# The experts' second layer with the hidden rows as the stationary operand

## The reference, cut to what matters

```python
a, g = jnp.split(xf @ We1[e] + be1[e], 2, axis=-1)
act = a * gelu(g)
yE  = act @ We2[e] + be2[e]          # the second layer, the place of the change
yr  = jnp.einsum('end,ne->nd', yE, w) # w: two weights of a row, the rest zero
x   = x + layernorm(ys + yr)
```

## Time and profile before

| what | us |
|---|---|
| three executions | 1189.19 median, 1187.93 to 1189.62 |
| the profiled execution, span | 1189.8 |
| PE busy | 1035.2 (87%) |
| DVE busy | 833.9 (70%) |
| ACT busy | 746.2 (63%) |
| POOL busy | 631.6 (53%) |
| 822 to 1091 us (pairs): PE, DVE, ACT busy | 268.29, 170.21, 173.46 of 269.00 |
| 1104 to 1130 us (singles): PE, DVE, ACT busy | 21.41, 18.47, 18.37 of 26.00 |

### The profile page before, as it was taken

The page is one execution under the profiler, slowest core; times in us unless marked ns, Lnnn a source line. Parts: engine busy times, 40 slices in busy tenths (PEclk is TensorE's granted clock), DMA queues, the critical chain, the costliest instruction groups (busy, mean ns, idle before and its releaser), DMA issues. The chain is left out here.

```text
span 1189.8 us, 31490 instructions
## 1 busy us (share of the span) xinstructions
PE 1035.2 (87%) x8446; PEld 597.5 (50%) x8446; DVE 833.9 (70%) x2411; ACT 746.2 (63%) x1311; POOL 631.6 (53%) x1184
## 2 busy tenths in 40 slices
PE   4689998898899898998777999866999999999875
PEld 3543333333333333332245665535888888888732
DVE  7587777777777777776768898532666666666737
ACT  4677767777767767775655566413666666666716
POOL 3246666666666666664422777771444444444344
PEclk9799999999999999998996899878999999999988
DMA  8313333333332333333243111112222222221166
GB/s 222 86 56 97 94 94 94 105 92 90 90 107 86 97 93 100 94 98 104 81 127 130 54 55 55 55 55 71 65 60 62 64 61 64 64 65 51 46 220 211
DMA packets 135606, 107.47 MB, mean 90 GB/s; under 512 B 32203, under 2 KB 127874, under 8 KB 135538
## 3 DMA queue, kind: packets, MB, share of 16 engines
q1 hardware_dynamic: 124722, 87.45, 26.1%
q0 software_dynamic: 8544, 17.78, 4.2%
q10 hardware_dynamic: 2272, 1.45, 0.4%
HBM read 55.96 MB, written 50.69 MB: 90 GB/s over the span
## 5 line engine op out<-in xcount | busy, mean ns | idle before, releaser
L1536 DVE TENSOR_REDUCE maxima<-ps 128x8 f32<-128x1024 f32 x320 | 384.3, 1222 | 125.4 <-PE ps L1159 111.1
L911 ACT ACTIVATE pT_area<-ps 128x1024 f32<-128x1024 f32 x320 | 327.7, 1026 | 143.6 <-PE ps L1190 143.0
L699 POOL TENSOR_SCALAR_AFFINE_SELECT pT_area<-pT_area 128x256 f32<-128x256 f32 (+1 forms) x448 | 190.8, 440 | 109.3 <-ACT pT_area L911 107.4
L801 POOL DMA_INDIRECT ys_dram<-quad_area,place_cur x139 | 133.1, 957 | 192.5 <-issue 136.6
L1231 PE MATMUL ps<-pT_area,quad_area 128*32 128x512 f32 (+3 forms) x2048 | 190.6, 446 | 0.0
L791 POOL DMA_INDIRECT xs_dram<-quad_area,idx_cur x128 | 123.0, 961 | 77.6 <-issue 75.2
L1190 PE MATMUL ps<-quad_area 64*128 64x512 bf16 (+3 forms) x1024 | 124.9, 301 | 37.3 <-DVE maxima L1536 34.7
L1398 PE MATMUL ps<-quad_area 128*128 128x256 f32 (+1 forms) x456 | 129.8, 367 | 6.3 <-issue 4.5
L1399 PE MATMUL ps<-quad_area 128*128 128x256 f32 (+1 forms) x456 | 128.3, 363 | 0.0
L1159 PE MATMUL ps<-quad_area 61*128 61x128 bf16 (+2 forms) x1792 | 126.4, 243 | 0.0
L1019 ACT ACTIVATE xnT<-ps,be_cur 128x256 f32<-128x256 f32 (+1 forms) x228 | 94.6, 448 | 47.6 <-PE ps L1399 47.3
(11 more groups left out here) (237 smaller groups left out, 1593.0 us busy)
## 6 DMA issues: line engine op xcount, KB each, us to landing
qk_dram<-split_area SPq DMA_DIRECT2D x192, 128.0 KB, 2.3
quad_area<-qk_dram SPq DMA_DIRECT2D x256, 96.0 KB, 2.3
row_area<-xs_dram SPq DMA_DIRECT2D x63, 132.0 KB, 2.1
pT_area<-ys_dram SPq DMA_DIRECT2D x16, 512.0 KB, 5.3
pT_area<-in_L_ffn_We SPq DMA_DIRECT2D x12, 384.0 KB, 6.1
out_dram<-pT_area SPq DMA_DIRECT2D x7, 512.0 KB, 2.9
xs_dram<-row_area SPq DMA_DIRECT2D x5, 528.0 KB, 4.2
split_area<-in_L_ffn_We SPq DMA_DIRECT2D x12, 192.0 KB, 3.6
```

What stands on the lines that cost most here:

```text
L699: return pool.affine_select(out=blocks, in_=blocks, compare_op=ALU.is_ge, fill=0.0, base=0, pattern=[[0, count], [1, P]], channel_multipli ...
L801: pool.indirect_dma_start(ys_dram, at, ys[:, ns % 2, h, :], None).then_inc(s_yst[ns % 2], 16)
L911: act.activation(pT[:, gs % 2, n, :], ps[:, bank:bank + 2, :].rearrange("p a b -> p (a b)"), ACT.Exp).then_inc(s_exp, 1)
L1536: dve.tensor_reduce(to, ps[:, bank:bank + 2, :].rearrange("p a (j k) -> p a j k", k=P), AX, ALU.max).then_inc(s_mxf, 1)
```

## The change

The operands of the second layer are exchanged. `hidT` (128 columns of it, one half of the tile) is now stationary and a 128 x 128 piece of `w2_cur` moves, so the result has rows on partitions at once. A pair takes six products of 128 columns instead of three of 256, a single three of 128. The two transposes of a pair, ACT's copy to `ysT` and `ysT` itself are gone; banks 6 and 7 (`Y_BANKS`) hold the results of alternate tiles.

With rows on partitions the bias is a row that is the same on all of them. `be2_all` holds the twelve rows on all 128 partitions, loaded by one broadcast DMA of 6 KB for each partition behind the expert weights; a new DVE copy brings the tile's row to `be2_cur`. `weigh` is DVE's new last step on a result: an addition of the bias (PSUM to SBUF, L1842 of the changed kernel), a wait until that is finished, and a product with the weights (SBUF to SBUF, L1844). `weigh(n-2)` stands ahead of the register load and of both copies, where before the product stood behind them. `beT` and `be_cur` lose a column, and `yT` moves to make room.

```diff
+            sp.dma_start(be2_all, a["L0_ffn_be2"].rearrange("(o e) c -> o (e c)", o=1).broadcast_to([P, E * C])).then_inc(s_we, 16)
...
-                if 0 <= ns - 1 < ROUTED:
-
-                    act.wait_ge(s_yeT, n)
-                    w = width(ns - 1)
-                    act.activation(ysT[:, (ns - 1) % 2, 0:w], ps[:, YT_BANK, 0:w], ACT.Identity,
-                                   bias=be_cur[:, (ns - 1) % 8, 6:7]).then_inc(s_yeTsb, 1)
...
                     pe.wait_ge(s_w2c, n)
-                    ge(pe, s_yeTsb, n - 1)
+                    ge(pe, s_yeb, n - 2)
                     for k in range(CHUNKS):
                         pe.wait_ge(s_hide, CHUNKS * (n - 1) + k + 1)
-                        last = pe.matmul(ps[:, YT_BANK, 0:w], w2_cur[:, par, k * P:(k + 1) * P], hidT[:, par, k, 0:w],
-                                         start=(k == 0), stop=(k == CHUNKS - 1))
-                    last.then_inc(s_yeT, 1)
-                if 0 <= ns - 2 < ROUTED:
-
-                    pe.wait_ge(s_yeTsb, n - 1)
-                    ge(pe, s_yesb, n - 2)
-                    for h in range(halves(ns - 2)):
-                        last = pe.transpose(ps[:, Y_BANK, h * P:(h + 1) * P], ysT[:, ns % 2, h * P:(h + 1) * P], ident[:])
+                        for h in range(halves(ns - 1)):
+                            last = pe.matmul(ps[:, Y_BANKS[par], h * C:(h + 1) * C], hidT[:, par, k, h * P:(h + 1) * P],
+                                             w2_cur[:, par, k * C:(k + 1) * C], start=(k == 0 and h == 0),
+                                             stop=(k == CHUNKS - 1 and h == halves(ns - 1) - 1))
                     last.then_inc(s_ye, 1)
...
-                    ge(dve, s_yeT, n - 1)
+                if 0 <= ns - 2:
+                    weigh(ns - 2, n - 2)
+                if ns < ROUTED:
+                    ge(dve, s_ye, n - 1)
                     e = dve.value_load(etile[0:1, bass.ds(n, 1)], min_val=0, max_val=E - 1)
                     dve.tensor_copy(w2_cur[:, par, :], we2[:, bass.ds(e * HR, HR)]).then_inc(s_w2c, 1)
-                if 0 <= ns - 2:
-
-                    par, h = ns % 2, halves(ns - 2)
-                    dve.wait_ge(s_ye, n - 1)
-                    wait_apart(dve, s_wt, 5 * n - 5, s_passed)
-                    if ns >= 4:
-                        dve.wait_ge(s_yst[par], stored(ns - 4, n - 4))
-                    dve.tensor_tensor(ys[:, par, 0:h], ps[:, Y_BANK, 0:P * h].rearrange("p (h c) -> p h c", h=h),
-                                      weight_cur[:, (ns - 2) % 4, 0:h].rearrange("p (h o) -> p h o", o=1).broadcast_to([P, h, C]),
-                                      ALU.mult).then_inc(s_yesb, 1)
+                    dve.tensor_copy(be2_cur[:, par, :], be2_all[:, bass.ds(e * C, C)]).then_inc(s_b2c, 1)
+
+            def weigh(ns, n):
+
+                par, h = ns % 2, halves(ns)
+                to, w = ys[:, par, 0:h], weight_cur[:, ns % 4, 0:h]
+                bias = be2_cur[:, par].rearrange("p (o c) -> p o c", o=1).broadcast_to([P, h, C])
+                dve.wait_ge(s_ye, n + 1)
+                wait_apart(dve, s_b2c, n + 1, s_passed)
+                wait_apart(dve, s_wt, 5 * n + 5, s_passed)
+                if ns >= 2:
+                    dve.wait_ge(s_yst[par], stored(ns - 2, n - 2))
+                dve.tensor_tensor(to, ps[:, Y_BANKS[par], 0:C * h].rearrange("p (h c) -> p h c", h=h), bias, ALU.add).then_inc(s_yeb, 1)
+                wait_apart(dve, s_yeb, n + 1, s_passed)
+                dve.tensor_tensor(to, to, w.rearrange("p (h o) -> p h o", o=1).broadcast_to([P, h, C]), ALU.mult).then_inc(s_yesb, 1)
```

More of the change, by code:

```diff
@@ L59 @@
 XS_BANKS = (4, 5)
-YT_BANK, Y_BANK = 6, 7
+Y_BANKS = (6, 7)
 PICK_STEPS, BOTH_STEP, PLACE_STEPS = 13, 12, 10
@@ L219, in build @@
         v_flat = v_all[:].rearrange("p t c -> p (t c)")
-        yT = v_flat[:, 1024:2048].rearrange("p (a t) -> p a t", a=2)
+        yT = v_flat[:, 512:1536].rearrange("p (a t) -> p a t", a=2)
+        be2_all = v_flat[:, 1536:1536 + E * C]
         gel = v_flat[:, 3072:4096].rearrange("p (a t) -> p a t", a=2)
@@ L256, in build @@
         outT = outT_area[:, 0:2 * T].rearrange("p (a t) -> p a t", a=2)
-        be_rows = sb("be_rows", [E * 7, P])
-        beT = sb("beT", [P, E, 8])
-        be_cur = sb("be_cur", [P, 8, 8])
+        be_rows = sb("be_rows", [E * 6, P])
+        beT = sb("beT", [P, E, 7])
+        be_cur = sb("be_cur", [P, 8, 7])
         rows_cur = quad_area[:, 0:DEPTH * NT * ROW].rearrange("p (a t c) -> p a t c", a=DEPTH, c=ROW)
@@ L265, in build @@
         hidT = quad_area[:, 0:2 * CHUNKS * RT].rearrange("p (a k t) -> p a k t", a=2, k=CHUNKS)
-        xsT, ysT = (quad_area[:, at:at + 2 * RT].rearrange("p (a t) -> p a t", a=2) for at in (2048, 3072))
+        xsT = quad_area[:, 2048:2048 + 2 * RT].rearrange("p (a t) -> p a t", a=2)
         ys = quad_area[:, 4096:4096 + 2 * RT].rearrange("p (a h c) -> p a h c", a=2, h=2)
@@ L355, in build @@
         s_xsT = sem("xsT_done"); s_xsTsb = sem("xsT_ready"); s_he = sem("expert_h_done"); s_ge = sem("expert_gelu_ready")
-        s_hide = sem("expert_hidden_ready"); s_w1c = sem("w1_cur_ready"); s_w2c = sem("w2_cur_ready"); s_yeT = sem("expert_yT_done"); s_yeTsb = sem("expert_yT_ready")
-        s_ye = sem("expert_y_done"); s_yesb = sem("expert_y_ready"); s_yst = [sem(f"ys_stored{n}") for n in range(2)]
+        s_hide = sem("expert_hidden_ready"); s_w1c = sem("w1_cur_ready"); s_w2c = sem("w2_cur_ready"); s_b2c = sem("b2_cur_ready")
+        s_ye = sem("expert_y_done"); s_yeb = sem("expert_y_with_bias"); s_yesb = sem("expert_y_ready"); s_yst = [sem(f"ys_stored{n}") for n in range(2)]
         s_wt = sem("weight_steps"); s_added = sem("picked_added"); s_sum = sem("routed_sums"); s_shift = sem("shift_ready"); s_normal = sem("normalised"); s_pick = [sem(f"rows_picked{n}") for n in range(3)]
@@ L938, in _ @@
             quad_steps(act, step)
-            act.wait_ge(s_w2, 176)
+            act.wait_ge(s_w2, 160)
             act.wait_ge(s_vcur, QUADS)
@@ L997, in _ @@
             act.activation(beT[:, :, 0:6], ps[:, BE_TURN, 0:6 * E].rearrange("p (e k) -> p e k", e=E), ACT.Copy)
-            act.activation(beT[:, :, 7], iota_f[:, ROUTED:ROUTED + E], ACT.Copy)
-            act.activation(beT[:, :, 6], ps[:, BE_TURN, 6 * E:7 * E], ACT.Copy).then_inc(s_beTsb, 1)
+            act.activation(beT[:, :, 6], iota_f[:, ROUTED:ROUTED + E], ACT.Copy).then_inc(s_beTsb, 1)
             skewed(act, shared)
-            act.wait_ge(s_we, 16 * 2 * E)
+            act.wait_ge(s_we, 16 * (2 * E + 1))
             def copy_w1(ns, n):
@@ L1300, in _ @@
             pe.wait_ge(s_exp, UNITS * QUADS)
-            pe.transpose(ps[:, BE_TURN, 0:7 * E], be_rows[:], ident[0:7 * E, 0:7 * E]).then_inc(s_beT, 1)
+            pe.transpose(ps[:, BE_TURN, 0:6 * E], be_rows[:], ident[0:6 * E, 0:6 * E]).then_inc(s_beT, 1)
             def shared(ns, n):
@@ L1810, in routed_as @@
                 dve.wait_ge(s_xs[ring], 32 * (n // 4 + 1) if isinstance(n, int) else 8 * (n - ring) + 32)
-                dve.tensor_scalar(second, second, be_cur[:, ns % 8, 7:8], None, ALU.is_equal).then_inc(s_wt, 1)
+                dve.tensor_scalar(second, second, be_cur[:, ns % 8, 6:7], None, ALU.is_equal).then_inc(s_wt, 1)
                 wait_apart(dve, s_wt, 5 * n + 1, s_passed)
@@ L1848, in _ @@
+            dve.wait_ge(s_we, 16 * (2 * E + 1))
             for par in range(2):
```

15 lines of the change are left out of this document (7 added, 8 removed).

## The result

The changed kernel took 1193.56 us (median of 19 runs, 1190.47 to 1198.33) beside 1189.4 us of the kernel before (median of 19 runs, 1183.74 to 1193.91). The ratio is 1.0030, 95% interval 1.0019 to 1.0042: slower by some 3.6 us, where 3.4 us faster was forecast. The profiled execution has a span of 1191.2 us.

What follows compares the result with a forecast made beforehand. PE was taken to bound the pairs, the PE-ACT loop the singles; DVE's new chain decides. Pairs -11.0, DVE's loop +1.0, singles +6.0, end +0.6: -3.4 us from 1189.2, so 1185.8 us, range 1179 to 1196.

Steps and rivals of the forecast that it cites:

- PE's step: Pairs: two transposes gone, six 256-column passes become twelve of 128; net -0.18 us, a step of 4.15 us, -11.0 us over 63 pairs.
- DVE's chain in the loop: Pairs in the loop: DVE's own operations and waits sum to 4.15 us, plus 0.05 for branch and register work: 4.20 us.
- The cover: Pairs: DVE's copy of the second-layer weights ends 1.4 us before PE wants it, so PE notices DVE's lag late.
- The singles' chain: Singles: DVE's chain of 3.42 us replaces today's 2.98 us step; 13 steps and the first two weighed pairs cost +6.0 us.
- the loop's price: Pairs in the loop: DVE falls back 0.05 us over 48 steps, 2.4 us, less 1.4 of cover: +1.0 us.
- the seven unrolled pairs behind it win the cover back: Pairs behind the loop: unrolled, DVE's chain is about 4.0 us, below PE's 4.15, so the 1.4 us of cover return.
- Elsewhere: nothing: Outside the expert stage's steps and end: the `be2` broadcast, `beT` and its copies were to cost nothing.
- My own formula: Whole kernel: -11.0 + 6.6, plus 48 us for each us of DVE's loop step above 4.15, less 1.4 of cover.
- The second rival: Pairs in the loop: DVE's chain is longer and takes over; slower than before from 4.27 us, 1193 us at 4.35; chance 0.26.
- The first rival: DVE's chain is shorter than counted; pairs give the whole -11.0, singles cost 0 to 5: 1178.5 to 1184; chance 0.22.
- the bare loads: Rival for PE's pair passes: six added weight loads aren't overlapped, pairs cost +31 us, about 1226 us; chance 0.02.
- the unshortened step: Rival: the pair's step isn't shortened, as ACT's rows or the stores end last; 1189 +- 2 us; chance 0.06.

## Why the prediction was wrong

**PE's step: right.** Forecast 4.15 us and -11.0 us over the pairs; measured 4.15 in the first 20 pairs and, where DVE never binds, -10.5 (-10.7 behind the first two steps). The twelve passes with twelve loads took 1.34 us as worked out. The Trainium skill's rule ("TensorE: Matmul & The Clock Gate", "Part 3: Packing small matmuls") that loads overlap only between different row groups does not hold for these passes: loads are busy 234.94 of 260.00 us beside a PE at 260.00. The same section also lets a load go ahead into a background weight buffer; the rows agree with that, and no run here tests it.

**DVE's chain in the loop: mechanism right, the register load too short.** Forecast 4.15 + 0.05 = 4.20, measured 4.24 on the mean of the loop (4.14 to 4.49 from step to step). Start to start, from the step above: 1.20 up to the first L1822 (1.17 forecast), 1.19 for the three (1.20), 0.56 from addition to product (0.57), 0.86 from product to copy (0.79), 0.28 and 0.14 as forecast; 4.23. The mis-sized term is the register load: I took 0.79 from a step where nothing stopped the sequencer ahead of it; behind the wait for the addition it is 0.86 in the loop, and the 0.05 that I had added for the loop covered only a part. Over 48 steps 0.04 us are 1.9 us. The cover was right: PE starts the second layer of tile 7 1.54 us behind the end of the weights' copy, and that of tile 18 0.13 us behind it, so 1.4 us were used up before PE's first long step, its 21st pair. The singles' chain was forecast at 3.42 and is 3.41 to 3.42.

**The wait between addition and product** costs 0.14 us behind the addition's end (902.29 against 901.73 + 0.42 = 902.15), where neighbours without a wait start 0.08 ahead of that end (L1829 to L1830). "VectorE: DVE Perf Modes", section "The DRAIN you can't avoid" of the Trainium skill, says of a semaphore between copies that it "costs nothing extra"; for this dependent pair the trace shows some 0.2 us.

**The steps that failed are the loop's price, "the seven unrolled pairs behind it win the cover back", the singles' mean step, and "Elsewhere: nothing".** My own formula gives -11.0 + 48 x 0.09 - 1.4 + 6.6 = -1.5 us for the measured 4.24, still no loss. Term by term (the first two rows behind the pairs' first two steps; the singles cut at DVE's last L1822 of a tile, which no change of order moves):

| us | forecast | measured |
|---|---|---|
| PE's shorter step | -11.0 | -10.7 |
| DVE's chain in the pairs | +1.0 | +3.5 |
| the stage's first two steps | 0 | +0.6 |
| DVE's lag at the pairs' end | 0 | +1.2 |
| the 13 single steps | +6.0 | +7.0 |
| the end of the stage | +0.6 | +0.6 |
| the last stage | 0 | +1.1 |
| sum | -3.4 | +3.3 |

- *DVE's chain in the pairs:* 258.16 us against 254.65 where DVE doesn't bind. 1.9 of the 2.5 us are the 0.04 us a step, the other 0.6 lie in the steps just ahead of the loop and behind it.
- *The cover isn't won back.* Behind the loop PE starts the second layer of tile 58 0.77 us behind its copy's end; then two written-out steps of DVE take 4.33 and 4.77 us, and from tile 60 on it is 0.05 to 0.06 (0.23 once). So DVE enters the singles with nothing in hand: its last L1822 of tile 62 starts 0.32 us behind the pairs' end, where before it started 0.88 us ahead of it.
- *The singles.* The undisturbed step is the forecast's 3.42, but the mean from copy to copy is 3.52, since 0.1 to 0.4 us of single disturbances (a step of 3.83 with an "issue" of 0.82 us in front of the copy) are now lost; before, DVE had slack that hid them.
- *The first two steps* vary by as much between profiles of the same code: 0.6 us that are no effect of the change.
- *The last stage.* TensorE's granted clock from 1141 to 1151 us is 0.65, and was 0.78 in the same window before. Its passes on the first picked rows take 1.0 to 1.2 us each at the lower level; before there are four such passes, in the changed kernel six, and the next picked rows' product starts 14.82 instead of 13.72 us behind the last scatter: these are the 1.1 us. Why the lower level lasts longer stays open. PE's spell of 2.77 us ahead of the last second layer, behind which that layer and the next products already run at the lower level, is one candidate:

```profile
1130.84 1.58 PE L1407 MATMUL ps<-outT_area,quad_area 128*128 128x128 f32 x6 [2.77 <-DVE outT_area L1829]
1132.22 2.95 PE L1422 MATMUL ps<-y_sb,ident 128*128 128x512 f32 x4
1142.02 2.08 PE L1425 MATMUL ps<-pT_area,ident 128*128 128x512 f32 x2 [6.85 <-DMA pT_area<-ys_dram]
```

But with the loop written out PE has the same spell and the next picked rows' product comes at 13.87 us, and with the product on ScalarE it has 1.52 us, the last second layer runs at the upper level, and that product still comes at 14.33.

**The rivals.** The loop's step lies in the forecast's own band (4.17 to 4.25) and the time doesn't: the band of the time was too narrow for what I gave to the singles and to the end. The second rival named the right engine and the wrong stretch: DVE made the kernel slower, but at 4.24 and not above 4.27 us, because the singles carried more. The first rival fell with the "issue" idles, the bare loads with the 1.34 us, and the unshortened step with the 4.15.

**The checks that I had named:** addition to product 0.57 (0.56), product to copy 0.79 (0.86), gelu waits nearly gone (2.3 of 32.2 us), singles at 3.4 us with PE waiting for the copy in each (14 waits, 12.6 us). All but the 0.86 came true, and the sign was still wrong: each check was on a step. Beyond the longer step, 4.8 us in six pieces lay outside the steps that I had counted or in their mean, beside a net of -1.5.

## What to carry over

When an engine's chain of waits on itself comes within a few hundredths of the bound, count what its slack used to hide (odd long steps, loop turns, a load that no longer runs ahead) as costs of their own. Put a register load and the copy that another engine needs ahead of any wait that has time: here the same instructions in another order made the pairs and singles 7.9 us shorter, 310.85 against 318.76. Slack that one stage uses up is missing in the next. And before moving work to another engine's queue, look at what will stand behind its wait: two moves that each gained were a loss together.

## What the runs showed of the hardware

- A register load on DVE is free when nothing stops the sequencer ahead of it (2.92 us a single step, no idleness in front of the copy), and costs an idle engine 0.34 to 0.48 us behind a waited instruction: 0.77 us from that instruction's start to the copy's in written-out code, 0.86 in the loop.
- The loop's register work costs DVE's chain 0.24 us a step (1.20 + 0.86 against 1.05 + 0.77), which nobody saw as long as DVE had slack.
- A 2.65 us idle spell ahead of TensorE's products on picked rows left them at 1.77 us instead of 1.02, in one profile; spells of 1.45 and 1.50 us left them at 1.13 and 1.12, as no spell did in another (1.13).
